# Gate and up weights of an expert tile fetched in one 384 KB transfer instead of two of 192 KB

## The reference, cut to what matters

```python
probs = jax.nn.softmax(logits, axis=-1)              # 8 experts
topw, topi = jax.lax.top_k(probs, TOP_K)             # TOP_K = 2
gate = jax.nn.silu(jnp.einsum('th,eih->eti', xf, w_gate))   # I = 352, H = 128
up   = jnp.einsum('th,eih->eti', xf, w_up)
down = jnp.einsum('eti,ehi->eth', gate * up, w_down)
out  = jnp.einsum('eth,te->th', down, combine)
```

## Time and profile before

| what | value |
|---|---|
| unprofiled runs | 476.52, 477.55 and 477.6 us, median 477.55 us |
| span of the profiled execution | 502.5 us, 13923 instructions |
| expert stage in the span | from the first gather at 354.4 us to the last scatter issued at 486.3 us |
| PE / DVE / ACT / POOL busy in the whole span | 85% / 64% / 59% / 41% |
| mean DMA rate over the span | 77 GB/s |

### The profile page before, as it was taken

One profiled execution on the slowest core, in us unless ns is written; L12 is line 12 of the kernel. 1 busy time (PEld: TensorE's weight loads), 2 busy tenths in 40 slices (PEclk: granted clock), 3 DMA queues, 4 the chain that ended last, 5 costly groups with the idle time before them and its releaser, 6 DMA issues.

```text
span 502.5 us, 13923 instructions
## 1 busy us (share of the span) xinstructions
PE 426.8 (85%) x4047; PEld 349.0 (69%) x4047; DVE 323.5 (64%) x969; ACT 296.4 (59%) x876; POOL 207.0 (41%) x482
## 2 busy tenths in 40 slices
PE   3899999999999999999878998888788688869760
PEld 3576767777776777777557787787777577758650
DVE  6488888888888888888756888887222222223225
ACT  4688888888888888888758876322122122212223
POOL 1545455555555455554310000000466655666530
PEclk9999999999999999999999999977889978998875
DMA  6272111111111111110000000020655555555316
GB/s 181 66 265 63 41 41 32 42 31 42 31 42 34 39 42 31 42 31 10 2 1 1 1 2 0 1 85 1 193 171 181 158 149 147 178 159 168 110 31 247
DMA packets 31999, 38.86 MB, mean 77 GB/s; under 512 B 5952, under 2 KB 29184, under 8 KB 31712
## 3 DMA queue, kind: packets, MB, share of 16 engines
q1 hardware_dynamic: 29040, 33.33, 22.1%
q0 software_dynamic: 2496, 5.12, 3.1%
q10 hardware_dynamic: 432, 0.02, 0.1%
HBM read 33.80 MB, written 4.65 MB: 77 GB/s over the span
## 4 chain that ended last, share of the span: by engine, by line
PE 31%; another core or an unknown queue 5%; ACT 5%; DVE 5%; issue 3%; DMA 2%; POOL 0%; POOLq 0%; DVEq 0%; ACTq 0%; SPq 0%
PE PS L1091 13%; PE PS L1099 4%; PE PS L950 3%; PE PS L980 2%; PE PS L1083 1%; PE PS L996 1%; PE PS L1076 1%; PE PS L830 1%; ACT SE L471 1%; PE PS L987 1%; PE PS L963 1%; DMA Y<-y_table 1%; DMA XG<-x_table,IDX 1%; DVE xe L693 1%
## 5 line engine op out<-in xcount | busy, mean ns | idle before, releaser
L397 ACT ACTIVATE PR<-PS,nmax 128x257 f32<-128x257 f32 x256 | 118.1, 474 | 32.7 <-DVE nmax L584 32.6
L584 DVE TENSOR_REDUCE nmax<-PS 128x1 f32<-128x257 f32 x256 | 90.5, 416 | 18.3 <-PE PS L874 17.6
L804 DVE TENSOR_TENSOR H<-PS,SG 128x384 f32<-128x384 f32 x39 | 21.8, 558 | 77.6 <-PE PS L1091 32.3
L881 PE MATMUL PS<-I,PR 128*128 128x128 f32 x512 | 66.8, 274 | 0.0
L346 POOL DMA_INDIRECT XG<-x_table,IDX x39 | 38.0, 974 | 56.1 <-DVE IDX L798 44.5
L1091 PE MATMUL PS<-XGT,GC 128*128 128x128 f32 x234 | 38.6, 307 | 24.8 <-ACT XGT L524 21.1
L881 PEld LDWEIGHTS PS<-I,PR 128*128 128x128 f32 x512 | 58.1, 142 | 0.3 <-issue 0.3
L357 POOL DMA_INDIRECT y_table<-YS,IDY x39 | 38.6, 988 | 44.7 <-DVE YS L809 40.7
L300 POOL TENSOR_TENSOR O<-OM 128x64 f32<-128x64 f32 x64 | 20.5, 321 | 85.0 <-DVE OM L607 85.0
L529 ACT ACTIVATE SG<-PS 128x384 f32<-128x384 f32 x39 | 19.2, 491 | 60.7 <-PE PS L1091 52.7
L1091 PEld LDWEIGHTS PS<-XGT,GC 128*128 128x128 f32 x234 | 33.2, 214 | 28.3 <-ACT XGT L524 23.4
(11 more groups left out here) (191 smaller groups left out, 850.1 us busy)
## 6 DMA issues: line engine op xcount, KB each, us to landing
CR<-ctxT SPq DMA_DIRECT2D x64, 128.0 KB, 2.1
GC<-w_gate SPq DMA_DIRECT2D x39, 192.0 KB
UC<-w_up SPq DMA_DIRECT2D x39, 192.0 KB
Y<-y_table SPq DMA_DIRECT2D x4, 512.0 KB, 5.0
DW<-w_down SPq DMA_DIRECT2D x1, 1536.0 KB, 6.1
NAMES<-lanes SPq DMA_DIRECT2D x1, 1344.0 KB, 8.9
X<-x SPq DMA_DIRECT2D x4, 256.0 KB, 4.4
x_table<-xe SPq DMA_DIRECT2D x4, 256.0 KB, 2.4
```

What stands on the lines that cost most here:

```text
L397: a.activation(PR[:, j % 2, gr, 0:S], src, ACT.Exp, bias=bias, accum_out=rsum[:, j % 2, gr:gr + 1]).then_inc(exped, 1)
L584: v.tensor_reduce(nmax[:, gr:gr + 1], bank[gr][:, 0:S], AX.X, ALU.max, negate=True).then_inc(max_ready, 1)
L881: ins = t.transpose(bank[4 + ch][:, 128 * gr:128 * gr + 128], PR[:, j % 2, gr, KC * ch:KC * ch + KC], I128[:, :])
```

## The change

One tile `GU` of 4 slots of (2, 384) columns takes the place of the rings `GC` and `UC`, with the same total size. In DRAM the gate and up weights of one expert lie side by side in `w_pair`, so that each partition's part of a pair is one run of 3072 bytes where there were two of 1536 bytes. SP issues one transfer per tile instead of two, and it waits for the up matmuls of tile s-4 alone. PE waits for the pair once, ahead of the gate matmuls; the wait ahead of the up matmuls falls away.

```diff
-        GC, UC = sb("GC", [128, WRING, IP]), sb("UC", [128, WRING, IP])
+        GU = sb("GU", [128, WRING, 2, IP])
...
-        gate_in, up_in = ([sem(f"{w}_in{n}") for n in range(WRING)] for w in ("gate", "up"))
+        pair_in = [sem(f"pair_in{n}") for n in range(WRING)]
...
                 if s >= WRING:
-                    sp.wait_ge(c["gate"], s - WRING + 1)
-                sp.dma_start(GC[:, s % WRING, :], w_gate[:, bass.ds(own[s], IP)]).then_inc(gate_in[s % WRING], 16)
-                if s >= WRING:
                     sp.wait_ge(c["up"], s - WRING + 1)
-                sp.dma_start(UC[:, s % WRING, :], w_up[:, bass.ds(own[s], IP)]).then_inc(up_in[s % WRING], 16)
+                sp.dma_start(GU[:, s % WRING, :, :].rearrange("p a n -> p (a n)"), w_pair[:, bass.ds(own[s] * 2, 2 * IP)]).then_inc(pair_in[s % WRING], 16)
...
                 t.wait_ge(c["xg_copied"], s + 1)
-                for name, w, bk, in_w in (("gate", GC, s % 2, gate_in), ("up", UC, 2 + s % 2, up_in)):
-                    t.wait_ge(in_w[s % WRING], 16 * (s // WRING) + 16)
+                t.wait_ge(pair_in[s % WRING], 16 * (s // WRING) + 16)
+                for name, half, bk in (("gate", 0, s % 2), ("up", 1, 2 + s % 2)):
                     if s >= 2:
                         t.wait_ge(c["silu"] if name == "gate" else c["hidden"], s - 1)
                     for n in range(IC):
-                        ins = t.matmul(bank[bk][:, 128 * n:128 * n + 128], w[:, s % WRING, 128 * n:128 * n + 128], XGT[:, s % 2, :],
+                        ins = t.matmul(bank[bk][:, 128 * n:128 * n + 128], GU[:, s % WRING, half, 128 * n:128 * n + 128], XGT[:, s % 2, :],
```

More of the change, by code:

```diff
@@ L38, in build @@
 def build(nc, x, ctxT, ctx_last, wq, wk, wv, wo, bo, w_dqT, w_kv, w_uqT, w_ukT, w_uvT, w_qr, w_out, raw_delta,
-          w_router, w_gate, w_up, w_down, ident, head_mask, cos_pos, sin_pos, own_sequence, expert_rank, routing, lanes, x_table, y_table, out):
+          w_router, w_pair, w_down, ident, head_mask, cos_pos, sin_pos, own_sequence, expert_rank, routing, lanes, x_table, y_table, out):
     held = ExitStack()
@@ L1154 @@
         "w_router": a(L0_ffn_w_router).T,
-        "w_gate": padded(a(L0_ffn_w_gate)).transpose(2, 0, 1).reshape(D, E * IP),
-        "w_up": padded(a(L0_ffn_w_up)).transpose(2, 0, 1).reshape(D, E * IP),
+        "w_pair": np.concatenate([padded(a(w)).transpose(2, 0, 1) for w in (L0_ffn_w_gate, L0_ffn_w_up)], axis=2).reshape(D, E * 2 * IP),
         "w_down": padded(a(L0_ffn_w_down).transpose(0, 2, 1)).reshape(E, IC, 128, D).transpose(2, 0, 1, 3).reshape(128, E * IC * D),
```

## The result

The changed kernel is slower: 482.01 us at the median (477.07 to 487.49, 7 runs) against 477.6 us (475.71 to 479.87, 7 runs). The ratio is 1.0066, with a 95% interval of 1.0037 to 1.0096. A forecast of no change was wrong, and 482.01 lies above the stated range. A second series of the same kernel (run e4) gave 483.08 us and 1.0104 (1.0051 to 1.0157).

The account below looks back on a forecast made before the run. POOL's issue rate, 2.57 us per tile, was taken to bound the expert stage. Terms 0 (steady state) + 0.1 (start) + 0 (SP) gave 477.65 us from 477.55, forecast as 477.5 us, range 473 to 480.

Parts of the forecast that it names:

- The pace: Expert stage: POOL's gather and scatter issues set a floor of 2.57 us per tile, 100.2 us for 39 tiles.
- floor and lead-in: Expert stage: POOL's 100.2 us plus PE's one tile of lead-in, about 2.1 us; the profiled stage exceeded both by 25.0 us.
- SP, and the later request for the gate half: Expert stage: SP relieved of 0.2 to 0.4 us a tile, gate half requested 0.67 us later; both valued at 0.
- The landing of the pair: Steady expert stage: the 384 KB transfer lands in 4.4 us, within 6.98 us of room; value 0.
- The start: Start of the expert stage: first pair may land late for the first gate matmul; +0.1 us, bounds 0 and +0.8.
- The gathers: POOL's loop over the gather ring: up to 0.97 us delay per gather fits in 1.35 us of slack; value 0.
- The slower rival: Expert stage: the pair's transfer holds up gathers beyond the ring's slack; 480, at most 485 us; chance 0.14.
- The packet rule: DMA queues: engines alternate by packet, so a gather waits for one longer packet, 3072 bytes instead of 1536; sum still 0.
- advice to coalesce: Weight transfers: about 2 us fixed cost each, so the pair would land some 2 us sooner, but off the path.
- The faster rival: Expert stage: late increments come of DMA traffic and shrink with fewer transfers; 474.5 us, at most down to 471.5; chance 0.22.

Follow-up runs that it names:

- e4: The changed kernel again, no edit, as a control against the kernel before on the same chip: 483.08 us, ratio 1.0104.
- e1: The kernel before again, no edit, as the control with a new trace: 477.18 us, ratio 0.9993.
- e2: The changed kernel, but the pair comes in two issues of 192 KB, both after the wait for up: 476.35 us, ratio 1.0003 to the kernel before.
- e3: The changed kernel with gate and up apart in DRAM, one issue of 256 runs of 1536 bytes: 480.13 us, ratio 1.0066 to the kernel before.
- e8: The changed kernel issuing only the 192 KB gate half, multiplied twice, up weights left out: 476.35 us, ratio 0.9977 to the kernel before.
- e6: The kernel before with six slots for gathered rows instead of four: 472.9 us, ratio 0.9911.
- e7: The changed kernel with six slots for gathered rows instead of four: 474.11 us, ratio 0.9932 to the kernel before.

## Why the prediction was wrong, step by step

**The pace.** Right: the stage runs at POOL's 2.57 us per tile, in the kernel before with few gaps (95.7 us from the first to the last gather). The remark that the long stage of the first trace had 25.0 us over POOL's floor, where the span had 24.95 us over the median, pointed the right way, and I should have acted on it: it said that the trace was not one of the runs to be predicted. That the two figures agree so closely was luck. From the first gate matmul to the last scatter e1 has 98.8 us (360.8 to 459.6), less than the 102.3 us of floor and lead-in, because four gathers are issued before that matmul.

**SP, and the later request for the gate half.** Right, at nothing. The later request is in e2, at 1.0003. SP's relief no run tests by itself. SP issued each pair in 0.34 us (median 338 ns) and no row of the changed kernel shows a wait of PE for it.

**The landing of the pair.** I took 4.4 us from the rows of 256 and 512 KB. Measured in e4:

```profile
L265 SPq DMA_DIRECT2D GU<-w_pair x39: 333/338/352, 356.6 to 454.9; - x39
...
DMA to landing us min/median/max: 3.1/3.7/5.4
```

Even 5.4 us fits into the room of 6.98 us. Right, though 4.4 us was too much for the typical one.

**The start.** I took +0.1 us, at most +0.8 us, for a first pair that comes late. No row of the changed kernel names the pair as what PE waited for. The first scatter follows the first gather by 9.5 us in e1 and 9.6 us in e4, so the term is near 0 there. In the first trace of the changed kernel it is 10.8 us and in e3 12.8 us. What differs is that the first twelve gate and up matmuls took 2.64 and 2.93 us there against 1.60 us in e1, that is, the clock, which my sum left out. With two transfers it is 9.1 to 10.7 us over all traces, with one 9.6 to 12.8 us, so whether the change makes a slow start more likely stays open.

**The gathers: the step that failed.** It read "The slack is 1.35 us, and 0.97 fits in. Value 0". I put one landing time, 3.5 us, into the loop, added the bound to it and compared the sum of 4.5 with the limit of 4.85. But the landing is a spread, and what counts is its tail. In the changed kernel the median is 3.6 to 3.7 us, well below the limit, and single gathers take 6.40 and 6.03 us in its first trace, 6.21 and 6.19 us in e4. Each such gather stops PE, then YS, then POOL, and POOL, the bound, never makes it up. So the 0.97 us that I called generous was too small as well: with two issues (e2) no gather with a known landing is above 4.3 us, some 2 us less:

```profile
DMA to landing us min/median/max: 2.5/3.1/4.3
```

The limit itself was too high. The chain of e1 has one late gather and what follows it:

```profile
400.56 4.46 DMA XG<-x_table,IDX
405.02 0.04 issue
405.06 0.33 PE PS L1083
405.39 0.06 issue
405.45 0.94 PE PS L1099 x6
406.39 0.02 issue
406.42 0.30 DVE YS L809
406.72 0.27 issue
406.99 0.99 POOL y_table L357
```

From the landing to the scatter are 1.97 us, where I had 1.58. POOL by itself would have come to this scatter five issues after the gather, which are 2.5 x 2.57 = 6.43 us, at 406.99. So 4.46 us is what the ring of four allows, not 4.85, and this one gather used it up without a loss.

The trace of before on which the step rested also hid how much of the slack was in use. One wait of 1.1 us for a gather stood in the earlier trace rows; in e1 there are ten with 5.2 us. I take it that PE had been held back by the late increments there, came to its gathers later and found them landed; no run shows that.

**The slower rival** was the right mechanism with the wrong weight, 0.14. Its condition was a landing of 4.85 us before the change. The latest gather on e1's chain took 4.46 us; it was the change that brought single gathers over the limit. Its price, at most 7.6 us, holds the measured 3.2 us (477.6 x 0.0066) to 5.0 us (at the 1.0104 of e4), but it was worked out as 0.97 us for every five tiles, and what happened is 2 us and more on a few. The lower clock after each long wait wasn't in it.

**The packet rule.** I brought up that engines take turns by packets and held one packet to be the price; the page cited was the Trainium skill, DMA: Bandwidth & Descriptors ("Queues, rings and completion order"). I took its packet for one run of bytes. The page means more by it: an engine "drains a whole packet (≈9-17 descriptors typical, spec ceiling ≤64)" of one queue before it switches. The packets of the earlier trace rows are single runs, 128 to a transfer. As an estimate from that page, with one descriptor for a run and the runs spread evenly over 16 engines, an engine has 8 runs of a transfer in the changed kernel and 16 in e3, so its whole share, 24 KB, could be one packet, and 12 KB in e2. Read like this the rule doesn't contradict the runs: the length of a run has no clear effect (e3 against e4) and the size of one transfer has (e3 against e2). No run here shows the turns themselves.

The same page's advice to coalesce ("Rules for kernel authors") is given for many small transfers, and the prediction drew from it that the pair would land some 2 us sooner than two transfers one after the other. 192 KB land in 2.5 us (e8) and 384 KB in 3.7 us (e4), less than twice 2.5. But the kernel before has both transfers in flight together, and the weights weren't what was waited for, so this gained nothing here.

**The faster rival** is out: no "remote" row in the stage in any of the later traces of either kernel.

**What stays open** is why one transfer in place of two matters to another queue. All gathers of the two traces that took over 4.85 us, past the first four, coincide with a fetch of instructions on another queue. The DMA view of the window of the 6.21 us gather (e4):

```profile
q1 hardware_dynamic: 361, 1.00, 56.1%
q0 software_dynamic: 136, 0.28, 18.9%
q8 instruction: 1, 0.02, 0.9%
```

In those two traces four in ten of the other gathers have a fetch in their window as well, so the coincidence alone doesn't settle it. More is in the increments. A transfer raises its semaphore sixteen times. Of the gather of 6.21 us fifteen increments came within 4.6 us and one at 6.21; of the other three of over 6 us fifteen came within 4.0 to 4.2 us. And in seven of the eight gathers over 4.85 us the last increment came 1.1 to 1.3 us after the end of the fetch's packet. In the kernel before such a fetch fell into the window of the gather of 4.46 us as well. It looks as if one of the 16 engines, held up by the fetch, carries its whole share of a weight transfer ahead of the gather. The single late increment is shown; that the fetch delays it, and more so beside a larger transfer, is argued from the times, and no run here leaves the fetches out.

## What to carry to other kernels

A transfer that nobody waits for still has a price if a transfer on the path shares the engines with it, so joining two hidden transfers can lose time, and the first thing to look at is who else is in flight. Compare the slack of a ring with the slowest landings, not with the median, and if it is short, lengthen the ring: with six slots for the gathered rows the loss of the change went. Two more slots also brought the kernel before 0.9%, by filling POOL's wait at the start of the stage; that is about as much as the split of the weights decides (0.7 to 1.0%). Before a sum is made from a trace, see whether its span is near the median of the runs; where it is 5% off, the waits in it may be those of that execution alone.

## What the runs showed of the hardware that I had not expected

- The landing of a 64 KB gather is later beside one larger transfer of another queue, at equal bytes per tile: with four slots the median is 3.1 us and the longest 4.3 us beside two transfers of 192 KB (e2), 3.6 to 3.7 us and 6.2 to 6.4 us beside one of 384 KB. With six slots the medians are 3.5 us (e6) and 3.9 us (e7). Beside one of 192 KB, with half the bytes, it is 2.7 us (e8).
- Of a gather that lands after over 6 us, fifteen of the sixteen increments come within 4.6 us and a single one late (four gathers of the changed kernel's two traces).
- At 1536 or at 3072 bytes per run, one transfer of 384 KB costs about the same: ratio 1.0066 (1.0036 to 1.0097) in e3, 1.0066 and 1.0104 (1.0051 to 1.0157) in the two series of the changed kernel.
- The waits of PE of 2.9 us in e4 are both followed by a stretch at 1.2 GHz: a granted clock of 0.50 over 391.3 to 394.7 us and over 452.8 to 456.1 us, where the kernel before (e1) has 1.00 from 359 to 459 us, with waits of at most 1.6 us.
- One execution of the kernel before was 25 us longer than the others, with waits for results of PE of up to 4.8 us booked under "remote". None of the other eleven traces shows such rows in its stage, and the cause isn't known.
